# Starting the marks after the keys alone, and gating scatters by zeroed pieces, in a four-layer graph network kernel

## The reference

```
neigh[dst] += edge_weight * x[src]          # 50000 edges, 256 features
y = concat(x, neigh) @ L0_gnn_weight + L0_gnn_bias
```

## Time and profile before

| | us |
|---|---|
| median of 3 runs | 4121.82 |
| the profiled execution | 4121.78 |
| its span in the profile | 4119.9 |
| TensorE busy in the span | 3064.7 (74%) |
| GpSimd busy | 2052.9 (50%) |
| VectorE busy | 2148.8 (52%) |
| ScalarE busy | 1554.6 (38%) |

### The profile page before, as it was taken

The page is one execution under the profiler, slowest core; times in us unless marked ns, Lnnn a source line. Parts: engine busy times, 40 slices in busy tenths (PEclk is TensorE's granted clock), DMA queues, the critical chain, the costliest instruction groups (busy, mean ns, idle before and its releaser), DMA issues. The chain is left out here.

```text
span 4119.9 us, 65409 instructions
## 1 busy us (share of the span) xinstructions
PE 3064.7 (74%) x16682; PEld 1859.7 (45%) x16683; DVE 2148.8 (52%) x5407; ACT 1554.6 (38%) x3260; POOL 2052.9 (50%) x2082
## 2 busy tenths in 40 slices
PE   1233776989888686668769966768765599899998
PEld 1122333567666333348644434644333344544544
DVE  2654001148888886563689956688656700301204
ACT  0176000068888464441026644026433600402303
POOL 1577777777770777731777770727776000000000
PEclk5555888999999798778989987879877699999999
DMA  9666633356775233436731112933352232232320
GB/s 398 227 190 182 188 112 94 97 128 139 135 206 140 86 106 105 137 101 243 219 106 27 27 27 70 291 110 106 105 162 86 96 95 90 70 96 64 95 83 32
DMA packets 328542, 521.94 MB, mean 127 GB/s; under 512 B 141966, under 2 KB 203111, under 8 KB 324677
## 3 DMA queue, kind: packets, MB, share of 16 engines
q1 hardware_dynamic: 217577, 309.55, 25.9%
q0 software_dynamic: 78896, 124.49, 11.2%
q10 hardware_dynamic: 31885, 85.88, 5.6%
HBM read 407.66 MB, written 115.58 MB: 127 GB/s over the span
## 5 line engine op out<-in xcount | busy, mean ns | idle before, releaser
L1027 PE MATMUL ps<-shared_sb,onehot 128*128 128x264 f32 (+1 forms) x1600 | 581.6, 472 | 170.7 <-DVE accum L2070 165.8
L1086 PE MATMUL ps<-score_sb,shared_sb 128*128 128x512 f16 (+1 forms) x3150 | 640.8, 364 | 17.3 <-DVE shared_sb L2099 17.2
L1305 ACT ACTIVATE onehot<-iota,drel 128x128 f32<-128x128 f32 x1248 | 381.3, 388 | 544.7 <-PE ps L950 326.9
L2070 DVE TENSOR_TENSOR accum<-accum,ps 128x264 f32 (+1 forms) x1248 | 527.7, 423 | 12.5 <-issue 5.4
L628 POOL DMA_INDIRECT t_w<-early_sb x391 | 399.4, 1021 | 221.9 <-DMA t_w<-accum 96.5
L1027 PEld LDWEIGHTS ps<-shared_sb,onehot 128*128 128x128 f32 x1600 | 288.8, 215 | 462.9 <-issue 212.8
L655 POOL TENSOR_SCALAR onehot<-iota,carry_d 98x512 bf16<-98x512 f32 x28 | 43.6, 1564 | 911.0 <-PE ps L1103 811.2
L1086 PEld LDWEIGHTS ps<-score_sb,shared_sb 128*128 128x128 bf16 x3150 | 308.8, 99 | 338.3 <-issue 11.4
L645 POOL DMA_INDIRECT t_adj<-counts,early_sb x391 | 385.3, 985 | 121.0 <-issue 118.9
L668 POOL DMA_INDIRECT shared_sb<-table,idx_a x384 | 364.0, 948 | 119.2 <-issue 116.6
L668 POOL DMA_INDIRECT score_sb<-table,idx_a x192 | 200.6, 1045 | 315.2 <-issue 148.4
(11 more groups left out here) (403 smaller groups left out, 5546.2 us busy)
## 6 DMA issues: line engine op xcount, KB each, us to landing
score_sb<-t_adj SPq DMA_DIRECT2D x105, 640.0 KB, 3.9
accum<-t_hot SPq DMA_DIRECT2D x208, 256.0 KB
t_w<-accum ACTq DMA_DIRECT2D x13, 3200.0 KB, 34.4
t_hot<-shared_sb SPq DMA_DIRECT2D x104, 256.0 KB
resid_sb<-t_w SPq DMA_DIRECT2D x25, 1024.0 KB
shared_sb<-t_key SPq DMA_DIRECT2D x98, 256.0 KB
t_adj<-accum ACTq DMA_DIRECT2D x40, 560.0 KB, 3.2
shared_sb<-t_adj SPq DMA_DIRECT2D x35, 640.0 KB, 9.2
```

The costliest lines, as they stand in the source:

```text
L1027: pe.matmul(ps[:, RING[(HU * h + u) % len(RING)], 0:w], onehot[:, h % 2 * HU + u, :], around[g][place(g, i, h)][:, u, 0:w], start=True, st ...
L1086: mm = pe.matmul(ps[:, 2 * (i % 3) + f, 0:w], h_gin[:, t, m, f * P:(f + 1) * P], ring["gin"][:, at % HOLD, c, 0:w], start=(t == 0 and m == ...
L1305: last = act.activation(onehot[:, h % 2 * HU + u, :], iota[:, 0:P], ACT.Abs, bias=drel[:, bass.ds(step + u, 1)], scale=-1.0)
L2070: dve.tensor_tensor(to, to, bank.unsqueeze(1), ALU.add).then_inc(step_acc, 1)
```

## The change

1. `FIRST` goes from 18 to 28: ScalarE joins ten quads later, and its loop over `t_adj` has 35 transfers in place of 40 (its size follows from `LOOPED`).
2. ScalarE issues the zeroes with two pieces in flight, the last piece of the matrix first: from the third on it waits until the piece two before has landed, and counts `w_zero` by one for each piece that has.
3. VectorE works out for each group of 8 quads how many pieces its scatters need (`zero_i`, with `last_of` and one small product on TensorE); six short instructions ahead of the first comparison.
4. GpSimd waits at the start of each group for its pieces: it reads the count into a register, and waits against it. The groups are eleven of 8 quads and one of 10.
5. SP no longer loads `x_pad` (ScalarE does, behind `x_cols`), waits for `t_key` alone before the loop, and writes `t_drel`, `t_hi` and `t_lo1` behind the loop.

```diff
-FIRST = 18
+FIRST = 28
+PIECES = WT // 2
+W_GROUP = 8
 @@ groups
-        for quads in [range(8 * m, 8 * m + 8) for m in range(10)] + [range(80, 89), range(89, QUADS)]:
-            w_order += [L0H * q + b for b in range(L0H) for q in quads if L0H * q + b < EDGES_T]
+        w_groups = [range(W_GROUP * m, W_GROUP * m + W_GROUP) for m in range(QUADS // W_GROUP - 1)]
+        w_groups.append(range(W_GROUP * len(w_groups), QUADS))
+        w_order = [L0H * q + b for quads in w_groups for b in range(L0H) for q in quads if L0H * q + b < EDGES_T]
+        w_first = [min(n for n, j in enumerate(w_order) if j // L0H == quads[0]) for quads in w_groups]
 @@ sync
-            put(hrows[:, :, 0:D], a["x_pad"].rearrange("(t p) d -> p t d", p=P), done("ld_xh"))
             sp.wait_ge(*count("adj_rows", 1))
             put(t_key[0:ET, :].rearrange("(q b) e -> q b e", b=EB), adj_t, done("key_out"))
             put(t_key[ET:S, :], no_key, done("key_out"))
-            sp.wait_ge(*count("keys", 1))
-            put(t_drel.rearrange("(b q) e -> q b e", b=SB), drow_b, done("key_out"))
-            sp.wait_ge(*count("keys", 2))
-            put(t_hi ...), put(t_lo1 ...), put(t_lo1 ...)
-            sp.wait_ge(*count("key_out", 48))
+            sp.wait_ge(*count("key_out", 32))
             with sp.Fori(0, QUADS // 2) as i:
 ...
+            sp.wait_ge(*count("keys", 2))
+            put(t_drel ...), put(t_hi ...), put(t_lo1 ...), put(t_lo1 ...)
 @@ gpsimd
-                pool.wait_ge(*count("w_zero", 16 * (WT // 2)))
+                pool.wait_ge(*count("need", 1))
                 for n, j in enumerate(w_order):
+                    if n == w_first[-1]:
+                        pool.wait_ge(*count("w_zero", PIECES))
+                    elif n in w_first:
+                        m = w_first.index(n)
+                        pieces = pool.value_load(zero_i[0:1, m:m + 1], min_val=1, max_val=PIECES)
+                        pool.wait_ge(done("w_zero"), pieces)
+                        pool.sem_inc(done("pool_go"), 1)
 @@ scalar
-            for part in t_w.rearrange("(k p n w) o -> k p n (w o)", k=WT // 2, p=P, w=W_ZERO):
-                act.dma_start(part, no_sums).then_inc(done("w_zero"), 16)
+            parts_w = t_w.rearrange("(k p n w) o -> k p n (w o)", k=PIECES, p=P, w=W_ZERO)
+            for n in range(PIECES + 2):
+                if n >= 2:
+                    act.wait_ge(attr_in[n % 2], 16 * (n // 2))
+                    act.sem_inc(done("w_zero"), 1)
+                if n < PIECES:
+                    act.dma_start(parts_w[(n - 1) % PIECES], no_sums).then_inc(attr_in[n % 2], 16)
             def compare(i, h):
 ...
             act.sem_inc(done("key_used"), FIRST + 2)
             act.sem_inc(done("same_act"), FIRST)
 ...
+            act.dma_start(hrows[:, :, 0:D], a["x_pad"].rearrange("(t p) d -> p t d", p=P)).then_inc(done("ld_xh"), 16)
             with act.Fori(FIRST // 2, QUADS // 2) as i:
 @@ vector
+            link(dve.tensor_scalar(last_of, iota[0:EQ, 0:QUADS // W_GROUP - 1], float(W_GROUP), float(W_GROUP - 1), ALU.mult, ALU.add))
+            link(dve.tensor_scalar(last_of, last_of, iota_p[0:EQ, :], None, ALU.is_equal))
+            link(dve.tensor_scalar(last_i, adj_d[:, EB - 1, P - 1:P], 8, None, ALU.logical_shift_right))
+            link(dve.tensor_copy(last_f, last_i))
+            link(dve.tensor_scalar(last_of, last_of, last_f, None, ALU.mult))
+            link(dve.tensor_scalar(zero_i[:, :], ps[:, 3, 404 + NT:404 + NT + QUADS // W_GROUP - 1], 2.0, float(PIECES), ALU.add, ALU.min))
```

More of the change, by code:

```diff
@@ L114, in build @@
         need_i = sb("need_i", [P, NT], I32)
+        zero_i = sb("zero_i", [P, QUADS // W_GROUP - 1], I32)
         lo_w = sb("lo_w", [P, 2, 2, P], BF16)
@@ L216, in build @@
         carry_at = flat_k[0:EQ, 8 * EB * P + 3 * EB:8 * EB * P + 3 * EB + 1].bitcast(I32)
+        last_i = flat_k[0:EQ, 8 * EB * P + 16:8 * EB * P + 17].bitcast(I32)
+        last_f = flat_k[0:EQ, 8 * EB * P + 20:8 * EB * P + 21]
+        last_of = flat_k[0:EQ, 8 * EB * P + 24:8 * EB * P + 24 + QUADS // W_GROUP - 1]
         weights_l1 = flat_k[:, 3456:3456 + 2 * GW].rearrange("p (c w) -> p c w", c=2)
@@ L281, in build @@
         key_in = [sem(f"key_in{h}") for h in range(2)]
-        in_four, so_far = attr_in + key_in, [0, 0, 16 * (QUADS // 2), 16 * (QUADS // 2)]
+        in_four, so_far = attr_in + key_in, [16 * len(range(h, PIECES, 2)) for h in range(2)] + [16 * (QUADS // 2), 16 * (QUADS // 2)]
         adj_in = [sem(f"adj_in{r}") for r in range(HOLD)]
@@ L340, in build @@
         counts_at = [2 * 16 * n for n in scattered]
-        w_order = []
-        for quads in [range(8 * m, 8 * m + 8) for m in range(10)] + [range(80, 89), range(89, QUADS)]:
-            w_order += [L0H * q + b for b in range(L0H) for q in quads if L0H * q + b < EDGES_T]
+        w_groups = [range(W_GROUP * m, W_GROUP * m + W_GROUP) for m in range(QUADS // W_GROUP - 1)]
+        w_groups.append(range(W_GROUP * len(w_groups), QUADS))
+        w_order = [L0H * q + b for quads in w_groups for b in range(L0H) for q in quads if L0H * q + b < EDGES_T]
+        w_first = [min(n for n, j in enumerate(w_order) if j // L0H == quads[0]) for quads in w_groups]
         quads_by = []
@@ L404, in _ @@
             put(t_key[ET:S, :], no_key, done("key_out"))
-            sp.wait_ge(*count("keys", 1))
-            put(t_drel.rearrange("(b q) e -> q b e", b=SB), drow_b, done("key_out"))
-            sp.wait_ge(*count("keys", 2))
-            put(t_hi.rearrange("(b q) e -> q b e", b=SB), hi_b, done("rows_out"))
-            put(t_lo1[0:S, :].rearrange("(b q) e -> q b e", b=SB), lo_rows, done("rows_out"))
-            put(t_lo1[S:S + UN, :], lo_rows[0:UN, 0, :], done("rows_out"))
             def on_each(t, first, n):
                 return t[bass.ds(first, n), :].rearrange("s e -> (s e)").unsqueeze(0).to_broadcast([P, n * P])
-            sp.wait_ge(*count("key_out", 48))
+            sp.wait_ge(*count("key_out", 32))
             with sp.Fori(0, QUADS // 2) as i:
@@ L422, in _ @@
                     sp.dma_start(wide_key[:, h, :], on_each(t_key, i * 2 * L0H + h * L0H, L0H)).then_inc(key_in[h], 16)
+            sp.wait_ge(*count("keys", 2))
+            put(t_drel.rearrange("(b q) e -> q b e", b=SB), drow_b, done("key_out"))
+            put(t_hi.rearrange("(b q) e -> q b e", b=SB), hi_b, done("rows_out"))
+            put(t_lo1[0:S, :].rearrange("(b q) e -> q b e", b=SB), lo_rows, done("rows_out"))
+            put(t_lo1[S:S + UN, :], lo_rows[0:UN, 0, :], done("rows_out"))
             put(weights_l1[:, :, 0:D], a["L1_gnn_W"].rearrange("(c p) n -> p c n", p=P), done("ld_w1"))
@@ L758, in _ @@
             pe.wait_ge(*count("adj_rows", 1))
+            pe.matmul(ps[:, 3, 404 + NT:404 + NT + QUADS // W_GROUP - 1], ones[0:EQ, :], last_of, start=True, stop=True)
             for b in range(EB):
```

## The result

The changed kernel takes 4126.59 us (median of 12 runs, 4121.49 to 4131.11), the kernel before 4119.6 us beside it (median of 12, 4112.95 to 4122.42): a ratio of 1.0018, with a 95% interval of 1.0011 to 1.0026. That is 7 us slower, just inside the 0.2% that I had named as what counts as no change. The prediction was 4135 us, with 4127 to 4152 as its range: its lower end lies 0.4 us above the median. On the 4121.82 us from which the prediction counts, the ratio gives 4129.2 us. The likeliest case was not the one that came, but the third rival (the register loads cost nothing, 4128.8 us).

The account below looks back on a forecast made before the run. ScalarE's credit behind the zero transfers was taken to hold the marks, and so the scatters. Zero loop 7.0 plus register loads 6.0 made 13.0 us on 4121.78: 4134.8 us, range 4127 to 4152.

Parts of the forecast that it names:

- The likeliest case: Whole kernel as computed: zero loop 7.0 us plus register loads 6.0 us, 4134.8 us; own range 4128 to 4142; chance 0.64.
- the third rival: GpSimd's group starts: register loads run beside the scatter before and cost nothing; +7.0 us stays, 4128.8 us; chance 0.16.
- What bounds the kernel: First 700 us: ScalarE's credit sets the marks' start, the eighth quad's sum sets the scatters, the last scatter the first layer's product.
- A fixed chain: After the last weight scatter: first layer's rest, then second layer's edge scores; a delay goes through to the end.
- The zero loop: ScalarE's credits now wait for the last landing, 114.5 us; first comparison 118.0, eighth scatter 149.3, 7.0 us later.
- That rival: Zero transfers: DMA engines run dry at 12 hand-overs, 1 us each, 4147 us; at most 4176; chance 0.14.
- The ten register loads: GpSimd's group starts: ten loads between scatters at 0.60 us each, 6.0 us; bounds 0 or 2.7, and 11.1 us.
- FIRST and the comparisons: VectorE: ten more quads with four comparisons, covered by the scatters, so nothing; 4 us without that cover.
- the rule that I put aside: VectorE/GpSimd shared ports: a 2-port VectorE instruction blocks GpSimd; ten more comparisons could cost up to 4.2 us.
- The groups and the moved transfers: Counted waits stop nothing and the tail stays; x_pad delays below 1 us; SP's tile loads 12 to 20 later, within 48 spare.
- The first rival: Marks' start: SP gets credits by other means, marks start with the keys; 4060 to 4097, say 4078 us; chance 0.06.

Follow-up runs that it names:

- credits first: The changed kernel with ScalarE's two credit lines (semaphore increments) moved ahead of its zero loop: 4072.36 us, ratio 0.9869; on the chip of 5,700 us, ratio 0.9898.
- constant waits: The changed kernel with a constant wait for all 13 pieces in place of the register loads: 4138.97 us, ratio 1.0021; on the chip of 5,700 us, 1.0009.
- credits at the last issue: The changed kernel with ScalarE's two credit lines inside the zero loop, directly behind the issue of the last piece: 4125.55 us, ratio 0.9998.
- before, credits first: The kernel before with ScalarE's two credit lines moved ahead of its zero loop, nothing else: 4123.56 us, ratio 0.9988; in another place, ratio 0.9991.
- counted waits out: The changed kernel with ScalarE's credit lines ahead of the zero loop and each group waiting for all 13 pieces by a constant: 4117.05 us, ratio 0.9967.
- four loads a group: The changed kernel with each register load made four times, 40 in all: 4138.68 us, ratio 1.0025; on the other chip, ratio 1.0002.

## Why the prediction came out as it did

**What bounds the kernel: right.** The marks' start sets the scatters, these the last products, and a shift goes through to the end: 7.2 us at the eighth scatter, 7.4 at the last, 7.3 at the ninth lot, 7.0 in the medians. "A fixed chain" was too strong for single traces, though: see "What a shift of the last scatter is worth" below.

**The zero loop: right, to 0.2 us.** I had the last landing at 114.5 us from 12.0 us less of traffic; the credit came at 114.4. First comparison 118.0, measured 118.06. Eighth scatter 149.3, measured 149.49. The experiments show the cause and not only the coincidence: with the credits behind the last issue the 7 us are gone, with the credits ahead of the loop 54 us more. There were no gaps between pieces: the DMA engines' share is 0.99 to 1.02 from 3 to 100 us. That rival did not occur.

**The ten register loads: the step that failed.** "I take VectorE's 0.60 [...]: 6.0 us". They cost about nothing: without them 1.0021, with them 1.0018; from the eighth scatter to the last the kernel before takes 508.0 us and the changed one 508.2. The sum of 13.0 us was thus nearly twice the 7.0 measured, and this one term is the whole difference. I had the right bound (0, "if it runs beside the scatter before it") and the right rival, and weighed it at 0.16 because the load would have to fit into the gap of 0.30 us. It need not fit there: the queue does it 5.4 to 8.4 us ahead of the scatter that waits for it, while earlier scatters are still to be done. The row that I priced by (VectorE's eight values, 0.60) was also the farther of the two: GpSimd's load takes 0.29 us, near SP's 0.27 of one value.

**FIRST and the comparisons: right for these, incomplete beside them.** Ten quads more with four comparisons cost nothing to be seen (508.0 against 508.2 us, as above; no run takes them out alone). But a neighbour of the rule that I put aside by the earlier trace rows does bear on this kernel, one stretch earlier than those rows: the Trainium skill (SBUF — State Buffer, "Who interferes with whom") says that a VectorE instruction with two inputs in SBUF contends with a GpSimd instruction that reads SBUF. By this trace it does, for the whole rest of the 2.27 us. Casts, with one input, lengthen scatters as well, to 1.54 and 1.68 us. Since the kernel before has the same long scatters (2.75 at the earlier trace rows), they cancel, and the forecast lost nothing by it.

**The groups and the moved transfers: right.** None of the counted waits stopped GpSimd, `x_pad` delayed nothing that was visible (one gap of 1.72 us at 175.42 is the longest behind the eighth scatter), and SP's later arrays were in time.

**The first rival** (marks that do start with the keys, 4078 us) did not come by this change, but its price was of the right size: with the two lines moved the kernel is 54 us faster, where the rival had 25 to 62 and 44 as its value. Its earliest first comparison would have been 39.8 us, VectorE's own date; 46.51 was measured, since SP's first key load leaves at 38.40 and it is 8.1 us from there to the comparison.

**What a shift of the last scatter is worth.** With the credits first the last scatter is 58.2 us earlier than before, the ninth lot only 46.2 (1289.21 against 1335.44) and the span 50.5. With the credits behind the last issue it is 5.2 us earlier, and the ninth lot 2.5 later. Part of it goes in the loop of the edge scores. Its reduction, of the kernel before, the changed one, the one with the credits first and the changed one with constant waits:

```profile
L1930 DVE TENSOR_REDUCE score_sb<-score_sb x104: 1285/1286/1289, 889.4 to 1333.2; 128x1088 f32 x104
```

```profile
L1955 DVE TENSOR_REDUCE score_sb<-score_sb x104: 1285/1286/1289, 900.4 to 1340.5; 128x1088 f32 x104
```

```profile
L1955 DVE TENSOR_REDUCE score_sb<-score_sb x104: 1285/1286/1289, 831.8 to 1287.0; 128x1088 f32 x104
```

```profile
L1952 DVE TENSOR_REDUCE score_sb<-score_sb x104: 1285/1286/1289, 899.3 to 1351.7; 128x1088 f32 x104
```

The same 104 steps take 443.8, 440.1, 455.2 and 452.4 us. The second and the fourth begin within 1.1 us of each other and differ by 12.3, so it is not the earlier start that makes the loop slower. The two traces beside the result have 443.8 and 440.1, the four from the chip of 4129.12 us 450.1 to 453.0, the two from the chip of 4126.46 us 447.5 and 455.2. The kernel before was traced in one place only, so what of this belongs to the chip and what to the single execution is open. VectorE's waits for the loads of the low codes, 40.9, 37.4 and 45.9 us between 890 and 1280 us in the first three, go the same way; nothing was run to tell the cause.

The ratios compare kernels on one chip and are free of this. The shift of the last scatter against the 650.3 us before, and the shift of the time that the ratio gives of 4120 us, with its interval:

| kernel | last scatter, us | time by the ratio, us |
|---|---|---|
| the changed kernel | +7.4 | +7.4 (4.5 to 10.7) |
| credits first | -58.2 | -54.0 (-60.2 to -47.8) |
| credits at the last issue | -5.2 | -0.8 (-4.5 to 2.9) |
| before, credits first | -5.3 | -4.9 (-8.7 to -1.2) |
| counted waits out | -14.6 | -13.6 (-19.0 to -8.2) |
| constant waits | +6.3 | +8.7 (4.5 to 12.4) |
| four loads a group | +8.1 | +10.3 (6.2 to 14.4) |

In six of seven the shift of the last scatter lies inside the interval. In the third it lies just outside, and why is open.

## What to carry to other kernels

When a wait is put into a loop, read what stands behind the loop on the same engine: here two semaphore increments, which touch nothing of the zeroes, held up the marks by 72 us and the kernel by some 61 (its ratio is 1.0018 with them behind the loop and 0.9869 ahead of it). An early start and finer waits may each be worth little and much together (the early start 0.3%, the finer waits without it nothing, both 1.3%), so such a pair should be judged as a pair, with its credits in place. And work that sits in front of an engine's main loop should only be moved after asking which queue waits for its result: an early result can release megabytes of loads into the very transfers that matter.

## What the runs showed of the hardware

A register load on GpSimd's queue (0.29 us, with 0.15 for the register operation) is done ahead of time, while indirect scatters of 0.96 us are in progress: 5.4 to 8.4 us ahead of the scatter behind it. Forty of them in ten groups left every gap between scatters at a group's start at 0.30 to 0.31 us.

A scatter that meets a VectorE subtraction of two 104x2048 arrays in SBUF (2.27 us) ends 0.83 to 0.84 us behind that instruction's end, so it takes 2.74 us instead of 0.96. Casts of 104x2048 elements (1.22 to 1.39 us) do the same: a scatter ended 0.82 us behind one. With that work out of the way there was no long scatter up to 260 us. For the subtractions this agrees with the section of the Trainium skill named above (SBUF — State Buffer, "Who interferes with whom").

Scatters issued while 3200 KB transfers fill the DMA engines take hardly longer than later ones; with the credits first it was 1.03 us each between 95 and 128 us and 1.01 between 200 and 300 (busy time and times of GpSimd; clock, DMA share and GB/s last), while VectorE waited 0.7 to 4.2 us for each key load between 102 and 129 us:

```profile
95.00:128.00 33.00, 25.69 (x25) 0.50 0.98 378
...
200.00:300.00 100.00, 77.13 (x76) 0.50 0.67 190
```
